# Folding LayerNorm into centred weights and moving sine and spike work to VectorE in a one-core hybrid block

## The reference, cut to what matters

```python
x = x + attn_a(layernorm(x), Wqkv, Wproj, bproj)      # LN1
x = x + ffn(layernorm(x), W_fc, W_proj)               # LN2
x = x + attn_b(layernorm(x), Wq, Wk, Wv)              # LN3, rotary, mask k <= q+1
x = x + ffn(layernorm(x), W_fc, W_proj)               # LN4

def layernorm(x): return (x - mean(x)) / sqrt(var(x) + 1e-5)
def ffn(x):
    y = square(relu(x @ W_fc.T)) @ W_proj.T
    # 5 steps: mem = 0.9*mem + y - reset; a spike where mem > 1
    return spikes_sum / 5
```

## Time and profile before

| | us |
|---|---|
| three runs | 203.21, 205.46, 206.30 (median 205.46) |
| profiled execution, device time | 205.26 |
| its span in the profile | 203.5 |
| busy: PE, PEld | 180.9, 159.5 |
| busy: DVE, ACT, POOL | 159.6, 114.2, 64.0 |

### The profile page before, as it was taken

The page is one execution under the profiler, slowest core; times in us unless marked ns, Lnnn a source line. Parts: engine busy times, 40 slices in busy tenths (PEclk is TensorE's granted clock), DMA queues, the critical chain, the costliest instruction groups (busy, mean ns, idle before and its releaser), DMA issues.

```text
span 203.5 us, 3973 instructions
## 1 busy us (share of the span) xinstructions
PE 180.9 (89%) x1264; PEld 159.5 (78%) x1264; DVE 159.6 (78%) x495; ACT 114.2 (56%) x265; POOL 64.0 (31%) x86
## 2 busy tenths in 40 slices
PE   7389969799989989598969999799999999999971
PEld 2189948597787868586868999699999999999961
DVE  2995685999897999988998787955879663974895
ACT  2269831659649188287836786364064945574260
POOL 7760054353372834232752105400010213012110
PEclk9969996999999999999999999999999999999998
DMA  5980000000000030300000000000000001000111
...
DMA packets 9825, 5.96 MB, mean 29 GB/s; under 512 B 447, under 2 KB 9422, under 8 KB 9806
## 3 DMA queue, kind: packets, MB, share of 16 engines
...
q10 hardware_dynamic: 720, 0.47, 0.8%
...
## 4 chain that ended last, share of the span: by engine, by line
PE 72%; DVE 12%; issue 7%; ACT 3%; POOL 3%; DMA 1%; DVEq 0%; ACTq 0%; POOLq 0%
PE bank_o L1099 14%; PE bank_m L1026 10%; PE bank_p L1087 7%; PE bank_s L910 6%; PE bank_s L912 5%; PE bank_s L911 5%; PE bank_h L910 3%; DVE xn L712 3%; PE bank_h L912 3%; PE bank_h L911 3%; PE bank_m L927 3%; PE bank_p L1062 2%; PE bank_h L962 2%; POOL rstd L457 2%; DMA id_sb<-in_ident 1%
## 5 line engine op out<-in xcount | busy, mean ns | idle before, releaser
L1099 PE MATMUL bank_o<-vone,pt 128*128 128x128 f32 x272 | 35.7, 275 | 0.9 <-DVE pt L845 0.5
L1099 PEld LDWEIGHTS bank_o<-vone,pt 128*128 128x128 f32 x272 | 33.6, 191 | 2.3 <-DVE pt L845 0.9
L1026 PE MATMUL bank_m<-wd,hid 128*128 128x128 f32 x256 | 32.9, 276 | 1.0 <-ACT hid L623 1.0
L1026 PEld LDWEIGHTS bank_m<-wd,hid 128*128 128x128 f32 x256 | 31.1, 192 | 2.2 <-issue 1.4
L612 ACT ACTIVATE relu<-bank_h 128x512 f32<-128x512 f32 (+2 forms) x44 | 20.5, 483 | 15.6 <-PE bank_h L912 12.7
L450 POOL TENSOR_SCALAR veps<-mom 128x4 f32<-128x4 f32 (+2 forms) x19 | 4.4, 231 | 62.9 <-DVE mom L694 62.8
L499 POOL TENSOR_TENSOR hid<-relu 128x512 f32<-128x512 f32 (+2 forms) x14 | 12.4, 892 | 37.0 <-ACT relu L612 37.0
L672 ACT COPY pt<-bank_p 128x512 f32<-128x512 f32 (+3 forms) x25 | 13.2, 528 | 16.2 <-PE bank_p L1087 13.8
L794 DVE SCALAR_TENSOR_TENSOR spiked<-y,spiked 128x512 bf16<-128x512 f32 (+2 forms) x34 | 19.1, 562 | 0.6
L712 DVE TENSOR_SCALAR xn<-xs,mom,rstd 128x128 f32<-128x128 f32 x54 | 17.2, 377 | 3.0 <-POOL rstd L457 2.8
L457 POOL TENSOR_TENSOR rstd<-veps,mhalf 128x4 f32<-128x4 f32 (+2 forms) x19 | 18.4, 966 | 1.4 <-POOL veps L450 0.2
...
## 6 DMA issues: line engine op xcount, KB each, us to landing
...
hid<-in_w_qkv ACTq DMA_DIRECT2D x1, 192.0 KB, 3.9
```

Of the source, the lines that this page charges most:

```text
L1026: last = nc.tensor.matmul(MB[:, C * t:C * t + C], hid[:, j % 2, m, P * t:P * t + P], wd[:, m, :], start=(m == 0), stop=(m == M - 1))
L1099: last = nc.tensor.matmul(O[:, C * (i % TG):C * (i % TG) + C], pt[:, n % 3, P * b:P * b + P], v[:, k, :], start=(k == 0), stop=(k == i))
```

## The change

Three things are changed, and all four lists of `PLAN` are written anew around them.

1. **LN2 to LN4 are folded.** The mean is taken out by the weights: `centre` on POOL makes the matrix I - 1/C (one instruction), and two new PE steps multiply it into `w_fc` and `w_rope` (512 and 384 columns, f32) in banks `H1` and `MB`. `w_hi` and `w_lo` then read these banks. `norm` and `nmr` are gone for LN2 to LN4, and `turn` transposes `xs` itself as soon as its rows are ready. The scale comes later: for the second attention in `qkv_copy` (a per-partition scale in the same two ACT instructions), for the FFNs in `y`. As relu and square are homogeneous of degree two, there the scale is 1/(var + eps), and `rstd` takes the power -1 for LN2 and LN4. `y` on ACT becomes one instruction for each tile of 128; on DVE it is one product with a broadcast scale. `stats` and `rstd` remain, but only `y` and `qkv_copy` wait for them.
2. **`sin` moves from POOL to DVE** (all four).
3. **All five comparisons of all jobs are on DVE** (`ON_DVE` is 5 throughout). `sign` and `count` are gone, and `xf` reads `spiked` directly.

Number of steps by engine, before and after: PE 275 and 272 (count 5 to 0, centre 0 to 2); ACT 198 and 185 (sign 10 to 0, norm 3 to 0, y 10 to 6, pt_copy 25 to 22, sq 18 to 25); DVE 249 and 257 (norm 16 to 4, spike 45 to 55, sin 0 to 4, y 1 to 5, w_lo 1 to 2, pt_copy 15 to 18, sq 12 to 11, rot 7 to 6); POOL 52 and 40 (sin 4 to 0, nmr 3 to 0, sq 14 to 8, w_lo 2 to 1, centre 0 to 1, rot 1 to 2).

The diff, cut to its core, with the parts of the new lists that the text speaks of:

```diff
-ON_DVE = [3, 3, 3, 3, 3, 5, 5, 5, 5, 5, 5]
+ON_DVE = [5] * 11
...
     "pe": """
+turn-0-0 kv-0-0 turn-0-1 q-0 kv-0-1 kv-1-0 kv-1-1 turn-0-2 q-1 acc-0 turn-0-3 kv-2-0 kv-2-1 q-2 kv-3-0 acc-1 kv-3-1
+acc-2 q-3 acc-3 centre-1 ao-0 centre-2 ao-1 at-0 pr-0 at-1 turn-1-0 ao-2 f1-0-0 turn-1-1 f1-0-1 pr-1 f1-0-2 f1-0-3
...
+pt-15-3 f2-8-0 f2-8-1 pv-15-1 pv-15-2 pv-15-3 f1-9-2 f1-9-3 turn-3-5 f1-10-0 f1-10-1 f2-9-0 f1-10-2 f1-10-3 f2-10-0
...
     "dve": """
...
+spike-3-1 pt_copy-0-0 spike-3-2 spike-3-3 o-0 cos-1 sin-1 rot-1-0 rot-1-1 score_copy-2-0 row_sum-1 spike-3-4 qk_lo-1-0
...
     "pool": """
+vnext_zero ids centre rstd-0-0 rstd-0-1 w_lo-0 rstd-0-2 bias-0 rstd-0-3 rstd-1-0 bias-1 sq-0-0 bias-2 sq-0-2 rstd-1-1
...
+        def make_sin(eng, g):
+
+            eng.wait_ge(v_ready, TG * (g + 1))
+            eng.wait_ge(trig_in[g], 32)
+            if g:
+                eng.wait_ge(half_ready[0], g)
+                eng.wait_ge(half_ready[1], g)
+            eng.tensor_tensor(
+                rsin[:].rearrange("p t (a c) -> p t a c", a=2),
+                qk[:, g % 2].rearrange("p t (a c) -> p t a c", a=2),
+                sin_sb[:, g % 2].unsqueeze(2).to_broadcast([P, TG, 2, C]), ALU.mult).then_inc(*one(done["sin", g]))
...
-                    nc.gpsimd.tensor_tensor(rstd[:, n, ts], veps[:, n, ts], mhalf[:, 0:nt],
+                    nc.gpsimd.tensor_tensor(rstd[:, n, ts], veps[:, n, ts], (mone if n % 2 else mhalf)[:, 0:nt],
                                             ALU.pow).then_inc(rstd_ready[n], 1)
...
+                elif step[0] == "centre":
+                    pool.wait_ge(id_in, 16)
+                    nc.gpsimd.tensor_scalar(centre[:], id_sb[:], -1.0 / C, None, ALU.add).then_inc(centre_ready, 1)
...
+                    if k == 1:
+                        nc.scalar.copy(w_fc_sb[:], src)
+                    nc.scalar.copy(wh[:, o:o + n], src).then_inc(w_hi, 1)
...
-                    nc.scalar.copy(y[:, j % 2, 0:width], MB[:, 0:width]).then_inc(*one(done["y", j]))
+                    n, g, scale = scale_of(j)
+                    act.wait_ge(rstd_ready[n], g + 1)
+                    for t in range(JOBS[j][1]):
+                        last = nc.scalar.activation(y[:, j % 2, P * t:P * t + P], MB[:, P * t:P * t + P], ACT.Copy,
+                                                    scale=scale[:, t:t + 1])
+                    last.then_inc(*one(done["y", j]))
...
-                    nc.scalar.copy(qk[:, g % 2, t, :], bank[:, 0:2 * C])
-                    nc.scalar.copy(v[:, n, :], bank[:, 2 * C:3 * C]).then_inc(v_ready, 1)
+                    scale = rstd[:, 2, n:n + 1]
+                    nc.scalar.activation(qk[:, g % 2, t, :], bank[:, 0:2 * C], ACT.Copy, scale=scale)
+                    nc.scalar.activation(v[:, n, :], bank[:, 2 * C:3 * C], ACT.Copy, scale=scale).then_inc(v_ready, 1)
...
-                    nc.vector.tensor_copy(y[:, j % 2, 0:width], MB[:, 0:width]).then_inc(*one(done["y", j]))
+                    n, g, scale = scale_of(j)
+                    dve.wait_ge(rstd_ready[n], g + 1)
+                    nc.vector.tensor_tensor(
+                        y[:, j % 2, 0:width].rearrange("p (t c) -> p t c", c=C),
+                        MB[:, 0:width].rearrange("p (t c) -> p t c", c=C),
+                        scale.unsqueeze(2).to_broadcast([P, JOBS[j][1], C]), ALU.mult).then_inc(*one(done["y", j]))
...
+                if step[0] == "centre":
...
+                    nc.tensor.matmul(bank[:, 0:WEIGHTS[k][1]], centre[:], RAW[k], start=True, stop=True).then_inc(
+                        centred[k], 1)
+                    reader[bank.name] = (w_lo[k], 1)
...
-                    pe.wait_ge(*done["norm", n, g])
+                    if n == 0:
+                        pe.wait_ge(*done["norm", n, g])
+                    else:
+                        rows_ready(pe, n, g)
...
-                        last = nc.tensor.transpose(bank[:, C * t:C * t + C], xn[lane][:, j % 2, t, :], id_sb[:])
+                        last = nc.tensor.transpose(bank[:, C * t:C * t + C], xs[:, t0 + t, :] if n else xn[:, j % 2, t, :],
+                                                   id_sb[:])
```

More of the change, by code:

```diff
@@ L120 @@
     "pe": """
[L121 to L130, removed]
@@ L180 @@
-spike-10-0 spike-10-1 spike-10-2 spike-10-3 spike-10-4 xf-10
+stats-0-0 stats-0-1 norm-0-0 stats-0-2 lo-0-0 norm-0-1 stats-0-3 lo-0-1 k_phi-0-0 norm-0-2 k_phi-0-1 norm-0-3 lo-0-2
+q_phi-0 k_phi-1-0 k_phi-1-1 lo-0-3 k_phi-2-0 k_phi-2-1 q_phi-1 k_phi-3-0 q_phi-2 k_phi-3-1 diag q_phi-3 heads-0
+heads-1 w_lo-1 w_lo-2 x1-0 stats-1-0 lo-1-0 heads-2 lo-1-1 x1-1 stats-1-1 stats-1-2 sq-1-0 y-0 spike-0-0 spike-0-1
+x1-2 lo-1-2 heads-3 stats-1-3 sq-2-2 y-1 spike-0-2 spike-1-0 spike-1-1 spike-1-2 spike-1-3 spike-0-3 spike-1-4
@@ L223, in hybrid_block @@
         rstd = sb("rstd", 4, T)
-        nmean = sb("nmean", 4, T)
-        nmr = sb("nmr", 4, T)
         mhalf = sb("mhalf", TG)
-        xn = [sb(f"xn{k}", 2, TG, C) for k in range(2)]
+        mone = sb("mone", TG)
+        xn = sb("xn", 2, TG, C)
+        centre = sb("centre", P)
         xh = [sb(f"xh{k}", 2, W, dt=F32R) for k in range(2)]
@@ L363, in one @@
             return signal[0], 1
-        def on_act_before(norm, g):
-            return sum(engine_of["norm", norm, k] == "act" for k in range(g))
         def raw_used(eng):
@@ L540, in _ @@
                 if step[0] == "w_hi":
-                    o, n = WEIGHTS[step[1]]
-                    act.wait_ge((wa_in, wf_in, wr_in)[step[1]], 16)
-                    nc.scalar.copy(wh[:, o:o + n], RAW[step[1]]).then_inc(w_hi, 1)
-                elif step[0] == "norm":
-                    n, g = step[1:3]
-                    lane, j = lane_job(n, g)
-                    t0, nt = NORM_JOBS[n][g]
-                    act.wait_ge(nmr_ready[n], on_act_before(n, g) + 1)
-                    if j >= 2:
-                        act.wait_ge(xT_ready[lane], j - 1)
-                    for t in range(nt):
-                        last = nc.scalar.activation(
-                            xn[lane][:, j % 2, t, :], xs[:, t0 + t, :], ACT.Identity,
-                            bias=nmr[:, n, t0 + t:t0 + t + 1], scale=rstd[:, n, t0 + t:t0 + t + 1])
-                    last.then_inc(*one(done["norm", n, g]))
+                    k = step[1]
+                    o, n = WEIGHTS[k]
+                    src = RAW[0]
+                    if k == 0:
+                        act.wait_ge(wa_in, 16)
+                    else:
+                        act.wait_ge(centred[k], 1)
+                        src = (None, H1, MB)[k][:, 0:n]
+                    if k == 1:
+                        nc.scalar.copy(w_fc_sb[:], src)
+                    nc.scalar.copy(wh[:, o:o + n], src).then_inc(w_hi, 1)
                 elif step[0] == "hi":
@@ L680, in _ @@
                     t0, nt = NORM_JOBS[n][g]
[L681 to L688 removed]
+                    rows_ready(dve, n, g)
                     for t in range(t0, t0 + nt):
```

178 lines of the change are left out of this document (88 added, 90 removed).

## The result

| | before | after |
|---|---|---|
| four runs each, alternating, median (us) | 205.56 (203.21 to 206.30) | 193.70 (192.12 to 194.15) |
| profiled execution, device time and span | 205.26, 203.5 | 194.15, 192.3 |
| busy: PE, PEld | 180.9, 159.5 | 178.1, 159.0 |
| busy: DVE, ACT, POOL | 159.6, 114.2, 64.0 | 152.2, 111.4, 46.8 |

The ratio is 0.9445, 95% interval 0.9341 to 0.9550. Forecast were 196.1 us and a range of 190.5 to 202.5. A run more than 1.5% above the fastest of its kernel, at a lower granted clock, is left out of every comparison; of the kernel with the link put back three of four runs (207.91 to 208.49 us) are such.

A forecast was written before the change was run, and what follows sets the result against it. Dependences set the pace before 40 us, PE and DVE bound 40 to 110, PE 110 to 192, the last tile's chain the end. Gains of 1.2 + 0 + 2.0 + 5.0 + 1.0 + 0 = 9.2 from 205.26 gave 196.1 us, range 190.5 to 202.5.

The forecast's parts named there:

- 0 to 26 us: Start of the kernel: `w_lo-0` moved back and `lo-0-0` ahead of `norm-0-1` gain 1.2 us, bounds 0 and 1.4.
- The centring: 26 to 40 us: new centring matmuls, 1.8 us, set against `q-3` moved ahead; 0 together, from 0.4 gained to 1.0 lost.
- The link behind `x1-0`: 26 to 40 us: the way from `x1-0` to `f1-0-0` shrinks by 4.0 us; gain 2.0, bounds 1.0 and 2.5.
- 40 to 110 us: Middle, PE and DVE both near their limit: fewer PE waits and less DVE work gain 5.0 us, bounds 2.5 and 7.2.
- 110 to 192 us: Stretch where PE is full: fourth sine and half rotation leave the last `tqk` path; gain 1.0 us, bounds 0 and 1.3.
- DVE holds the middle: Rival: PE waits for DVE instead of `rot`, so 40 to 110 us yields nothing; 201.1 us, chance 0.20.
- nothing comes through: Rival: `w_lo`, `MB` and new lists take up the early gains, only 1.0 us of last `tqk` comes; 204.3 us, 0.09.
- PE had slack from 110 us on: Rival: the 6.6 us in which PEld is not busy from 110 us are slack and get filled; 189.5 us, chance 0.06.
- Slower, as DVE's queue is the bound: Rival: from 40 to 110 us all added DVE work counts in full, 10.1 us; 210.7 us, chance 0.03.
- theory two: From the follow-up experiments: the change buys shorter dependences, and these make it possible to put more on DVE.
- Theory one: From the follow-up experiments: the parts of the change add up, each by its own price.
- theory three: From the follow-up experiments: what counts is how much DVE has to do.

The follow-up runs named there:

- the kernel with the link put back: Changed kernel with 38 unread tiles redone on DVE behind each row-writing step and its statistics, the LN2 to LN4 transposes waiting for them: 204.39 us, a single run.

## Why the prediction was right, step by step

The time came out at 193.7 for 196.1, inside the range and its likeliest case. The mechanism was right: shorter links and an unblocked DVE, with the gain made before PE is full. The nearness of the sum is partly luck, as terms missed in opposite directions: the start was 2.6 us worse in the profiled execution, and the rest 4.5 better.

*0 to 26 us, taken as 1.2: the step held, the gain did not last.* The first `kv` starts 1.1 us earlier (0.6 in the changed kernel run again). But `x1-0` ends 1.4 us later than before. The granted clock from 9 to 18 us is 0.62, where the kernel before shows 0.81. Part of the loss is work that moved ahead of `x1-0` (`q-3`, the two centring products). `norm-0-1` was not cheaper either: it took 2.18 us beside POOL's `bias` addition of 128x512 (1.27 us), where the old one took 1.08. In the changed kernel run again the clock was 0.81 there, the norm took 1.11 us ahead of that addition, and `x1-0` ended at 32.83, as early as before. So the term was 0 in one execution and -1.4 in the other, never 1.2. The prediction priced the start by dependences alone, and left out the clock and what a norm meets on POOL; how the 1.4 us divide between these two stays open.

*The centring, 0: as expected.* The two products took 1.02 and 0.81 us at 27.25 and 29.10, next to work that waited anyway. The estimate of 1.8 us for 896 columns agrees with these durations, 1.83 in sum; the next matmul starts 0.86 and 0.64 us behind them, so that in the row they cost 1.5.

*The link behind `x1-0`, taken as 2.0: its size was exact, its worth a little above.*

```profile
33.57 0.68 DVE L776 TENSOR_TENSOR xs<-bank_p,xs 128x512 f32<-128x512 f32 x1
...
34.30 0.44 PE L953 MATMUL bank_m<-id_sb,xs 128*128 128x128 f32 x2 [0.36 <-DVE xs L776]
...
34.78 0.37 ACT L567 CAST xh<-bank_m 128x256 fp32r<-128x256 f32 x1 [0.21 <-PE bank_m L953]
...
35.18 0.42 DVE L726 TENSOR_TENSOR xl<-bank_m,xh 128x256 fp32r<-128x256 f32 x1
...
35.75 0.35 PE L921 MATMUL bank_h<-xh,wh 128*128 128x256 f32 x1
```

From 34.25 to 35.75 are 1.5 us, against 5.5: 4.0 less, as worked out. Not all of that is gained: `pr-1` and `at-2` stood ahead of `f1-0-0` and now stand behind it, 1.2 us by their starts in a full row (0.80 and 0.36), 1.5 by the prediction's price. So the link is worth 2.8 us, or 2.5 by that price, its upper bound. At `f1-0-0` the lead is 2.7 us (-1.4 and 4.0), of which 1.2 is this work put off.

*40 to 110 us, taken as 5.0 with PE's terms at 7.2.* Stages cut at the same steps, `f1-0-0` to `tqk-2`, before and after:

```profile
38.40:105.60 67.20, 59.88 (x405) 51.02 (x406) 59.94 (x172) 43.64 (x106) 31.32 (x32) 1.00 0.06 17
```

```profile
35.75:97.67 61.92, 58.16 (x404) 51.65 (x405) 54.00 (x161) 43.94 (x106) 21.93 (x27) 1.00 0.06 18
```

The stage is 5.3 us shorter, and by the lists it holds 1.3 us more FFN work ahead of `tqk-2` and the 1.2 us of `pr-1` and `at-2`. So for the same work it is 7.8 us shorter, above the upper bound of 7.2. PE's idle time fell from 7.3 to 3.8 us. The mechanism was right; the term was sized too low because the prediction let DVE's share of the time (0.895) limit it. DVE's work fell by 5.9 us here, not 3.2, and its share to 0.87, and as the runs show that share was not the limit: 8 us of idle work cost 1.6, and 9 us less of it (`sign` and `count` back) did not help.

*110 to 192 us, taken as 1.0.* From `tqk-2` to `tqk-3` 26.8 us became 25.9, and PE's idle 1.3 us there (26.75 less 25.46 busy) became none, although the new stage holds 1.1 us more work. That makes 1.9 us for the same work, where 1.3 was the upper bound; the wait was met, the term a little low. *Tail, 0:* `turn-3-5` to the end took 9.3 and takes 9.0. The terms as measured, -1.4, 2.8, 7.8, 1.9 and 0, make 11.1 of the 11.2 us.

*The `y` on ACT, counted at nothing: right, with a wrong price.* Each instruction takes 0.371 us and not 0.273, so four of them cost 1.5 us, but no wait of PE names `y`.

*The rivals.* "DVE holds the middle" and "nothing comes through" are out: `tqk` waits fell by 3.2 us. "PE had slack from 110 us on" is out too: from 135 to 182 us PE was full in both, with PEld at 43.66 and 44.37 of 47.00 us, and the stage from `tqk-3` on got no shorter beyond the work moved out of it. "Slower, as DVE's queue is the bound" is what happens without the fold: 216.5 us, with DVE busy for only 60.01 of the 70 us from 40 to 110 and PE waiting 7.8 us for norms behind LN1's.

**What the study adds to the prediction.** It summed the parts as if each had its own price. With the runs as a table (us; the fold's row has the new lists too, and the new lists without the fold were not run, so what follows is said of the fold and its lists together):

| | neither | sine on DVE | five comparisons | both |
|---|---|---|---|---|
| no fold | 205.4 | 202.6 | 217.6 | 216.5 |
| fold | 201.9 | 198.9 | 198.9 | 194.0 |

Moving the sine is worth 1.1 to 4.9 us in any company (1.1, between sets on two chips, is near nothing). The five comparisons are worth +3.0 and +4.9 with the fold and -12.1 and -13.9 without. The fold is worth 3.5 us while three comparisons leave room, and 22.5 with the fourth and fifth on DVE; that these make its queue late is what the one chain above shows. So theory two is the one that the runs bear out. Theory one fails by the sums, and theory three by the two runs with 8 us more and 9 us less of DVE work. Open stays how the 12 to 14 us divide between waits as such and the lower clock behind them (0.90 and 0.93 from 40 to 110 us in those two kernels, 1.00 in all that were fast), and whether another list would carry five comparisons without the fold; the two tried did not.
